# Attention scores from two exact float32 parts on two row halves of the array, late expert weights from a copy, and all orders written anew

## The chip, the core and the metric

The kernel runs on one core of one Trainium2 chip, as one program. The metric is device time in microseconds (us) of one execution. The core has TensorE for matrix products (PE in the profile, with its weight loads as PEld), VectorE (DVE), ScalarE (ACT), GpSimd (POOL), and SyncE (SP), whose queue issues nearly all DMA transfers. Matmul results land in PSUM, which has eight banks of 512 float32 numbers per partition.

## The reference

Input x has 32 sequences of 256 tokens of width 128. Two layers follow each other, with adaptive shift, scale and gate from a small conditioning product per sequence:

- Layer 0: an RWKV block (layernorm, token shift, three projections, the WKV recurrence over time, output projection, then a squared-relu channel mix with 512 hidden units), then a dense MLP 128 to 512 to 128.
- Layer 1: attention with 16 query heads of width 8 and 4 key/value heads, rotary positions, and a softmax over all 256 tokens of the sequence, then a mixture of 8 experts (128 to 512 to 128) of which each token takes two.

The part that the change is about:

```python
scores = jnp.einsum('bthd,bshd->btsh', q, k) * scale
probs = jax.nn.softmax(scores, axis=2)
```

## The kernel before, in words

The work is cut into 16 chunks of two sequences (512 tokens). Each step of a chunk has a name: A and E are the RWKV block, B the dense MLP and the q, k and v projections, C and G attention, R the router, S the slot numbers of the experts and the scatter to them, M the experts, K the gather and the last sum. The tokens of four groups of chunks (5, 5, 4 and 2 chunks) are sorted into tiles of 128 slots, each of which belongs to one expert: 156 tiles in all. The last 62 of them, the late tiles, run as steps W on TensorE (W_t turns four tiles, W_u is the first product, W_d the bias and the second), the others as M.

The order of the work on each engine is written out by hand, as a table ORDER at the file's end: five long lists of step names, one for each engine's queue. Every engine walks its list, and semaphores tie the lists together. An engine never overtakes its own list, so a step that waits holds up everything behind it.

PSUM banks are given out in rings. The ring of attention has the banks 3, 4 and 5, which C_s, C_mt and G_s take in turn; before a step writes its bank, TensorE waits until the bank's last user was read (`vacated`).

Scores need float32 accuracy. Each of q and k is split by ScalarE and GpSimd (B_split, L889, three bf16 copies a chunk, and B_sub, L735, two subtractions between them) into three bf16 parts, stored to scratch (B_stq) and loaded again for one sequence at a time (C_ld), so that each of the 9 pairs of parts of the 8 channels has a row of its own: 72 rows. For every sequence (a unit, 32 in all), TensorE then runs 16 steps C_s: two matmuls of 256 columns each (L1196), one for a head, rows 0 to 71 of the array. VectorE takes the negated row maximum from PSUM (L1581). The maxima are split into three bf16 parts too (C_mp), turned (C_mt), copied out of PSUM by ScalarE (L895) and moved by three small transfers (C_row, L576) into rows 72 to 74 of the q operand, against rows of ones in the k operand. So the second score product, 16 steps G_s of one matmul of 512 columns on 75 rows (L1212), gives the turned scores with the maximum subtracted, of which ScalarE takes the exponential (L903). G_pv (L1228) multiplies the probabilities with v: four heads side by side, each in a tile of 128 rows by 32 columns of the array. Other matmuls that don't take the whole array are the bias products on 3 and 24 rows (L1017, L1041), the k projection (L1178) and C_mt (L1202).

The expert products are L1028 (W_u and M_u: four float32 matmuls of 128 columns), L1041 (the bias, 24 rows, bf16) and L1045 (W_d and M_d: again four float32 matmuls). A float32 matmul stands in the profile as two passes, so four of them are x8. SP loads a tile's weights (514 KB) with L633 from the input wexp. The slot buffers are filled with zeros by four large transfers (Z, L510).

## Time and profile before

| what | value |
|---|---|
| median of 3 runs | 1633.04 us (1629.73 to 1641.36) |
| span of the profiled execution (first to last instruction) | 1622.0 us |
| median of the runs less that span | 11.0 us |
| TensorE busy | 1353.9 us (83%), granted clock 0.909 of full speed |
| VectorE, ScalarE, GpSimd busy | 1095.2, 990.8 and 545.8 us (68%, 61%, 34%) |
| bytes moved | 217.68 MB |

For the profiled execution the profile gives the span; what lies around it is taken from the runs, as in the third row. A row of the timeline gives the start of a group, how long it took to its modelled end, its engine, line, operation and tiles, its form, and how many instructions it merges. "75*128 75x512 bf16" means weights on 75 rows by 128 columns, and a moving operand of 512 columns. Since matmuls are pipelined, their modelled ends lie behind the next one's start; the time from start to start says what a group takes of the engine.

### The profile page before, as it was taken

How to read it: one execution, taken by the hardware profiler on the slowest of the kernel's cores; microseconds unless marked ns; L12 is line 12 of the kernel's file. 1: busy time of each engine (PE TensorE's matmuls, PEld its weight loads, DVE VectorE, ACT ScalarE, POOL GpSimd, SP SyncE). 2: the span in 40 equal slices, each digit the busy share in tenths (PEclk: the TensorE clock that was granted, in tenths of full speed). 3: DMA queues.
4: the chain of work that ended last, by engine and by line, in shares of the span. 5: the costliest groups of instructions: out<-in, count | busy, mean ns of one | idle time of the engine just before them, and what ended most of it. 6: DMA issues, size and time to landing. Idle time of an engine off the chain costs nothing.

```text
span 1622.0 us, 26719 instructions
## 1 busy us (share of the span) xinstructions
PE 1353.9 (83%) x8354; PEld 866.5 (53%) x8354; DVE 1095.2 (68%) x2943; ACT 990.8 (61%) x2295; POOL 545.8 (34%) x589
## 2 busy tenths in 40 slices
PE   3466897889888888999999979899899998998681
PEld 1234454534445444666666644467566754687571
DVE  5568879788989898676876895967755754140113
ACT  1354765667676556877777766567568565555430
POOL 2123222313122475212112256435322134344335
PEclk7677998989999889999999998799999999999885
DMA  4012135142321424454544524256555556788772
GB/s 126 7 36 72 42 114 167 46 132 64 110 77 30 121 83 116 139 157 124 168 134 141 154 87 137 78 164 193 159 169 171 159 166 207 225 275 276 225 244 76
DMA packets 202037, 217.68 MB, mean 134 GB/s; under 512 B 17419, under 2 KB 167526, under 8 KB 199593
## 3 DMA queue, kind: packets, MB, share of 16 engines
q1 hardware_dynamic: 193704, 199.18, 41.0%
q0 software_dynamic: 8192, 16.79, 3.4%
q8 instruction: 68, 1.11, 0.3%
q14 instruction: 73, 0.59, 0.1%
HBM read 161.18 MB, written 53.94 MB: 133 GB/s over the span
## 4 chain that ended last, share of the span: by engine, by line
PE 43%; DVE 21%; issue 11%; ACT 8%; POOL 7%; DMA 6%; SPq 2%; POOLq 0%; ACTq 0%; another core or an unknown queue 0%; DVEq 0%
DVE cmx L1581 6%; PE bank L1228 5%; PE bank L1045 5%; PE bank L1028 5%; PE bank L1212 5%; PE bank L1196 4%; PE bank L1151 3%; PE bank L1124 2%; POOL kg L775 2%; DMA kg<-y_slots,sslot 2%; PE bank L1164 2%; PE bank L1013 2%; POOL bhs L775 2%; ACT wide L903 2%; PE bank L1140 2%
## 5 line engine op out<-in xcount | busy, mean ns | idle before, releaser
L1581 DVE TENSOR_REDUCE cmx<-bank 128x2 f32<-128x512 f32 x512 | 328.7, 684 | 97.4 <-PE bank L1196 89.3
L903 ACT ACTIVATE wide<-bank 128x512 f32<-128x512 f32 x512 | 280.0, 609 | 69.2 <-PE bank L1212 64.6
L1212 PE MATMUL bank<-wide 75*128 75x512 bf16 x512 | 174.9, 407 | 23.2 <-DVE cmx L1581 14.7
L1196 PE MATMUL bank<-wide 72*128 72x256 bf16 x1024 | 176.2, 283 | 20.6 <-DVE cmx L1581 15.6
L756 POOL DMA_INDIRECT x_slots<-sx,sslot x128 | 128.1, 1001 | 111.3 <-issue 46.9
L1196 PEld LDWEIGHTS bank<-wide 72*128 72x128 bf16 x1024 | 92.0, 101 | 124.7 <-issue 48.2
L1228 PE MATMUL bank<-wide,bva 128*32 128x512 f32 x1024 | 146.5, 646 | 9.9 <-ACT wide L903 5.7
L942 ACT ACTIVATE mH<-bank,mW 128x128 f32<-128x128 f32 x376 | 107.0, 371 | 57.8 <-PE bank L1028 50.9
L1028 PE MATMUL bank<-mT,mW 128*128 128x128 f32 x872 | 123.8, 287 | 17.0 <-DMA mW<-in_wexp 7.9
L1028 PEld LDWEIGHTS bank<-mT,mW 128*128 128x128 f32 x872 | 112.6, 199 | 36.3 <-issue 14.7
L775 POOL DMA_INDIRECT kg<-y_slots,sslot x88 | 85.9, 976 | 117.9 <-DMA kg<-y_slots,sslot 35.6
L1212 PEld LDWEIGHTS bank<-wide 75*128 75x128 bf16 x512 | 49.3, 104 | 131.1 <-ACT wide L903 60.1
L1045 PE MATMUL bank<-mW,mH 128*128 128x128 f32 x752 | 109.8, 289 | 0.0
L663 POOL TENSOR_TENSOR brs<-bvar,half 128x4 f32<-128x4 f32 x32 | 33.9, 1058 | 218.2 <-DVE bvar L1297 218.1
L1045 PEld LDWEIGHTS bank<-mW,mH 128*128 128x128 f32 x752 | 91.8, 192 | 6.3
L1151 PE MATMUL bank<-bh,w 128*128 128x512 f32 x128 | 81.2, 720 | 15.1 <-ACT bhs L879 8.0
L735 POOL TENSOR_TENSOR bqk<-bqk,bp 128x768 f32<-128x768 f32 x32 | 54.9, 1715 | 88.9 <-ACT bp L889 88.8
L879 ACT ACTIVATE bhs<-bank,col 128x512 f32<-128x512 f32 x64 | 44.0, 687 | 57.7 <-PE bank L1151 53.4
L949 ACT ACTIVATE mX<-bank 128x128 f32<-128x128 f32 x120 | 33.5, 279 | 73.3 <-PE bank L1045 66.1
L1124 PE MATMUL bank<-axk,fwk 128*128 128x512 f32 x128 | 70.2, 650 | 5.5 <-DVE axk L1300 5.3
L1603 DVE RECIPROCAL crs<-bank 128x16 f32<-128x16 f32 x64 | 16.2, 253 | 84.0 <-PE bank L1234 80.6
L1722 DVE TENSOR_SCALAR kg<-kg,rinfo 128x128 f32<-128x128 f32 x44 | 9.8, 285 | 91.9 <-DMA kg<-y_slots,sslot 91.8
(296 smaller groups left out, 2863.4 us busy)
## 6 DMA issues: line engine op xcount, KB each, us to landing
mW<-in_wexp SPq DMA_DIRECT2D x109, 514.0 KB
wide<-q_parts SPq DMA_DIRECT2D x32, 576.0 KB
inner<-in_wexp SPq DMA_DIRECT2D x31, 514.0 KB
wide<-in_wexp SPq DMA_DIRECT2D x16, 514.0 KB
mX<-x_slots SPq DMA_DIRECT2D x27, 256.0 KB
y_slots<-mX SPq DMA_DIRECT2D x27, 256.0 KB
q_parts<-bp SPq DMA_DIRECT2D x32, 192.0 KB
x_slots<-mH SPq DMA_DIRECT2D x2, 3072.0 KB, 10.9
```

Of the source, the lines that this page charges most:

```text
L756: pool.indirect_dma_start(out=x_slots[GROUP_OF[c]], out_offset=bass.IndirectOffsetOnAxis(ap=sslot[:, c, k, t:t + 1], axis=0), in_=sx[:, c ...
L775: pool.indirect_dma_start(out=kg[z][:, k, t, :], out_offset=None, in_=y_slots[GROUP_OF[c]], in_offset=bass.IndirectOffsetOnAxis(ap=sslot[: ...
L903: act.activation(cP[:, i % 8, :], bank[seat["G_s", i]][:, :], ACT.Exp, scale=SCALE).then_inc(S["c_p"], 1)
L942: act.activation(hidden[z][:, c * P:(c + 1) * P], bank[seat[k]][:, c * P:(c + 1) * P], ACT.Relu, bias=w_[:, FC * P + c:FC * P + c + 1]).th ...
L1028: ins = pe.matmul(ps[:, c * P:(c + 1) * P], weights[w_][:, c * P:(c + 1) * P], mT[:, q % 2, j * P:(j + 1) * P], start=True, stop=True)
L1045: ins = pe.matmul(ps[:, 0:P], hidden[z][:, c * P:(c + 1) * P], weights[w_slot(i)[0]][:, o:o + D], start=False, stop=(c == FC - 1))
L1124: pe.matmul(ps[:, :], fwk[:, j * P:(j + 1) * P], flat(axk[:, :, :]), start=True, stop=True).then_inc(S["e_fk"], 1)
L1151: pe.matmul(ps[:, :], w1[:, j * P:(j + 1) * P], bh[:, :], start=True, stop=True).then_inc(S["b_w1"], 1)
L1196: ins = pe.matmul(ps[:, j * T:(j + 1) * T], cQ[0:SROWS, z, h, tt * P:(tt + 1) * P], cK[0:SROWS, z, h // G, :], start=True, stop=True)
L1212: pe.matmul(ps[:, :], cK[0:KROWS, z, g, sc_ * P:(sc_ + 1) * P], cQ[0:KROWS, z, h0:h0 + 2, :], start=True, stop=True).then_inc(S["c_s2"], 1)
L1228: ins = pe.matmul(CO[32 * g:32 * g + 32, :], bva[:, c % 2, b * 2 + sc_, g, :], cP[:, (4 * i + g) % 8, :], start=(sc_ == 0), stop=(sc_ == 1))
L1581: dve.tensor_reduce(cmx[:, u % 2, tt, 2 * hp:2 * hp + 2], bank[seat["C_s", i]][:, :].rearrange("p (j t) -> p j t", j=2), AX_X, ALU.max, ne ...
```

## The change

- q and k are cut into two float32 parts instead of three bf16 parts. The first keeps the upper 20 bits of the word (VectorE, an AND with a mask, new step B_cut), the second is what is left (GpSimd, one B_sub). The three copies B_split on ScalarE are gone. The row maxima are cut in the same way (C_mp: two operations in place of four).
- The 4 pairs of parts take 32 rows of the array in place of 72 (34 in place of 75 with the maximum). They are read as float32r, one pass per matmul. Heads 0 to 7 lie on rows 0 to 33, heads 8 to 15 on rows 64 to 97. A step C_s or G_s is now a pair: it takes two banks of the ring and alternates matmuls between the two halves. There are 256 of each in place of 512; the number and size of the matmuls is the same, and so are the 512 reduces and 512 exponentials.
- All expert weights (1024 rows of 4112 bytes) are copied once, early, from the input to a scratch tensor w_late (new step I_wl on SP's queue), and the 62 late tiles load theirs from there.
- The q and k operands have an SBUF tensor of their own, qk, in place of a part of wide; the 8 extra weight buffers of the last group lie in both.
- The five lists of ORDER are new.

```diff
+CUTS = 2
+SROWS = CUTS * CUTS * HD
+KROWS = SROWS + CUTS
+HALF = H // 2
+KHALF = KV // 2
+LOW = P // 2
+CUT = -4096.0
...
+PAIRED = ("C_s", "G_s")
...
-            n = banks[k % len(banks)]
-            seat[s, i], before[s, i] = n, had.get(n)
-            had[n] = (s, i)
-            k += 1
+            for j in ((2 * i, 2 * i + 1) if s in PAIRED else (i,)):
+                n = banks[k % len(banks)]
+                seat[s, j], before[s, j] = n, had.get(n)
+                had[n] = (s, j)
+                k += 1
...
-        q_parts = scratch("q_parts", [UNITS * PARTS * P, T], BF16)
-        k_parts = scratch("k_parts", [UNITS * PARTS * HD * KV, T], BF16)
+        q_parts = scratch("q_parts", [UNITS * CUTS * P, T])
+        k_parts = scratch("k_parts", [UNITS * CUTS * HD * KV, T])
+        w_late = scratch("w_late", [EXPERTS * P, WROW])
...
-        bp = sb("bp", [P, PARTS, QK], BF16)
+        bp = sb("bp", [P, CUTS, QK])
+        cutf = sb("cutf", [P, 1])
+        cuti = sb("cuti", [P, 1], I32)
+        cut = cuti[:, :].bitcast(U32)
...
+        qk = sb("qk", [P, NQ * WROW])
+        cQ = qk[:, 0:cQ_ROW].rearrange("p (s h t) -> p s h t", s=2, h=HALF)
+        cK = qk[:, cQ_ROW:cQ_ROW + cK_ROW].rearrange("p (s g t) -> p s g t", s=2, g=KHALF)
+        cQr, cKr = cQ.bitcast(F32R), cK.bitcast(F32R)
...
-        weights += [wide[:, k * WROW:(k + 1) * WROW] for k in range(WIDE)]
+        weights += [qk[:, k * WROW:(k + 1) * WROW] for k in range(NQ)]
+        weights += [wide[:, k * WROW:(k + 1) * WROW] for k in range(WIDE - NQ)]
...
+                    if s == "I_wl":
+                        sp.dma_start(w_late, a["wexp"]).then_inc(S["p_wl"], 16)
...
+                        for o in range(2):
+                            sp.dma_start(cQ[o * LOW:o * LOW + SROWS, z, :, :].rearrange("r h t -> r (h t)"),
+                                         q_parts[i * CUTS * P:(i + 1) * CUTS * P, :]
+                                         .rearrange("(r h) t -> r (h t)", h=H)[:, o * HALF * T:(o + 1) * HALF * T]
+                                         .unsqueeze(1).broadcast_to([CUTS * HD, CUTS, HALF * T])
...
+                        for o in range(2):
+                            sp.dma_start(cQ[o * LOW + SROWS:o * LOW + KROWS, z, :, :].rearrange("r h t -> r (h t)"),
+                                         cmT[o * H:(o + 1) * H, z, :]).then_inc(S[f"c_rows{z}"], 16)
...
-                        sp.dma_start(weights[k], a["wexp"][bass.ds(row, P), :]).then_inc(S[f"m_w{k}"], 16)
+                        if i == LATE_TILE:
+                            sp.wait_ge(S["p_wl"], 16)
+                        sp.dma_start(weights[k], (a["wexp"] if i < LATE_TILE else w_late)[bass.ds(row, P), :]
+                                     ).then_inc(S[f"m_w{k}"], 16)
...
-                        c, k = divmod(i, PARTS - 1)
-                        pool.wait_ge(S["b_p"], PARTS * c + k + 1)
-                        if k:
-                            pool.wait_ge(S["b_r"], i)
-                        pool.tensor_tensor(bqk, bqk, bp[:, k, :], ALU.subtract).then_inc(S["b_r"], 1)
+                        pool.wait_ge(S["b_p"], i + 1)
+                        pool.tensor_tensor(bp[:, 1, :], bqk, bp[:, 0, :], ALU.subtract).then_inc(S["b_r"], 1)
...
-                    if s == "B_split":
-                        c, k = divmod(i, PARTS)
-                        if k:
-                            act.wait_ge(S["b_r"], 2 * c + k)
-                        else:
-                            act.wait_ge(S["b_qk"], 2 * c + 2)
-                            if c:
-                                act.wait_ge(S["b_stq"], 64 * c)
-                        act.activation(bp[:, k, :], bqk, ACT.Copy).then_inc(S["b_p"], 1)
...
+                    if s in PAIRED:
+                        pair = [bank[seat[s, 2 * i + o]] for o in range(2)]
+                        for o in range(2):
+                            vacated(s, 2 * i + o)
+                    elif (s, i) in seat:
...
-                        u, m = divmod(i, MAXES)
+                        u, m = divmod(i, MAXES // 2)
                         z = u % 2
                         if m == 0:
                             pe.wait_ge(S[f"c_ldq{z}"], 64 * (u // 2 + 1))
-                        tt, hp = divmod(m, H // 2)
+                        tt, hp = divmod(m, HALF // 2)
                         for j in range(2):
                             h = 2 * hp + j
-                            ins = pe.matmul(ps[:, j * T:(j + 1) * T], cQ[0:SROWS, z, h, tt * P:(tt + 1) * P],
-                                            cK[0:SROWS, z, h // G, :], start=True, stop=True)
-                        ins.then_inc(S["c_s"], 1)
+                            for o in range(2):
+                                ins = pe.matmul(pair[o][:, j * T:(j + 1) * T],
+                                                cQr[o * LOW:o * LOW + SROWS, z, h, tt * P:(tt + 1) * P],
+                                                cKr[o * LOW:o * LOW + SROWS, z, h // G, :], start=True, stop=True)
+                                if j:
+                                    ins.then_inc(S["c_s"], 1)
...
+                        pp, sc_, g = m // 4, m // 2 % 2, m % 2
                         h0 = g * G + pp * 2
-                        pe.matmul(ps[:, :], cK[0:KROWS, z, g, sc_ * P:(sc_ + 1) * P], cQ[0:KROWS, z, h0:h0 + 2, :],
-                                  start=True, stop=True).then_inc(S["c_s2"], 1)
+                        for o in range(2):
+                            pe.matmul(pair[o][:, :], cKr[o * LOW:o * LOW + KROWS, z, g, sc_ * P:(sc_ + 1) * P],
+                                      cQr[o * LOW:o * LOW + KROWS, z, h0:h0 + 2, :],
+                                      start=True, stop=True).then_inc(S["c_s2"], 1)
...
+                    if s == "B_cut":
+                        dve.wait_ge(S["b_qk"], 2 * i + 2)
+                        if i:
+                            dve.wait_ge(S["b_stq"], 96 * i)
+                        dve.tensor_scalar(bp[:, 0, :].bitcast(U32), bqk.bitcast(U32), cut[:, 0:1], None,
+                                          ALU.bitwise_and).then_inc(S["b_p"], 1)
...
-                        dve.tensor_copy(cmp[:, :, 0, :], x_).then_inc(S["c_mp"], 1)
-                        dve.wait_ge(S["c_mp"], PARTS * i + 1)
-                        v(dve.tensor_tensor(cr1[:, :, :], x_, cmp[:, :, 0, :], ALU.subtract))
-                        v.wait()
-                        dve.tensor_copy(cmp[:, :, 1, :], cr1[:, :, :]).then_inc(S["c_mp"], 1)
-                        dve.wait_ge(S["c_mp"], PARTS * i + 2)
-                        dve.tensor_tensor(cmp[:, :, 2, :], cr1[:, :, :], cmp[:, :, 1, :],
-                                          ALU.subtract).then_inc(S["c_mp"], 1)
+                        dve.tensor_scalar(cmp[:, :, :, 0, :].bitcast(U32), x_.bitcast(U32), cut[:, 0:1], None,
+                                          ALU.bitwise_and).then_inc(S["c_mp"], 1)
+                        dve.wait_ge(S["c_mp"], CUTS * i + 1)
+                        dve.tensor_tensor(cmp[:, :, :, 1, :], x_, cmp[:, :, :, 0, :], ALU.subtract).then_inc(S["c_mp"], 1)
...
-        I_ld A_ld I_ldw I_ldx*16 I_st0 I_ldx*5 A_ldm I_ldx*4 A_ldg I_ldx*4 I_st1 I_ldx*2 A_ld I_ldx B_ldm A_ldm
+        I_ld I_ldw I_ldx*13 A_ld I_ldx*3 I_st0 I_ldx*4 A_ldm I_ldx*9 I_st1 I_ldx A_ldm I_ldx A_ldg A_ld A_ldm
```

Two places show how instructions moved. The first is TensorE's list in the middle of the program, around the channel mix of a chunk (axk, fwk: its first product; mT, mW and mH: expert tiles; ident with bz, ez or cctx: transposes; cos_: attention output; cmp: row maxima; wide with bva: probabilities times v). L1196 (C_s) and L1212 (G_s) read wide. Before:

```order
L1178 MATMUL bank<-bh,wkr 32x256 x2
L1212 MATMUL bank<-wide 128x512 x2
L1196 MATMUL bank<-wide 128x256 x2
L1028 MATMUL bank<-mT,mW 128x128 x4
L1228 MATMUL bank<-wide,bva 32x512 x4
L1212 MATMUL bank<-wide 128x512
L1184 MATMUL bank<-wvT,bh 128x32 x4
L1212 MATMUL bank<-wide 128x512 x2
L1041 MATMUL bank<-eb,which 128x128
L1045 MATMUL bank<-mW,mH 128x128 x4
```

The same kind of place afterwards; L1213 (C_s) and L1234 (G_s) read qk:

```order
L1213 MATMUL bank<-qk 128x256 x4
L1146 MATMUL bank<-fwr,axr 128x128 x4
L1213 MATMUL bank<-qk 128x256 x4
L1140 MATMUL bank<-axk,fwk 128x512
L1213 MATMUL bank<-qk 128x256 x4
L1140 MATMUL bank<-axk,fwk 128x512
L1213 MATMUL bank<-qk 128x256 x4
L1140 MATMUL bank<-axk,fwk 128x512
L1221 MATMUL bank<-ident,cmp 32x128 x2
L1213 MATMUL bank<-qk 128x256 x4
```

Score matmuls still stand singly between float32 groups, now as pairs of steps: four matmuls of 256 columns, or two of 512, at a time.

The second is SP's list where the first maxima go out (C_row, cmT). am, bm, ax, x_b are the loads and stores of other chunks. Before:

```order
L562 DMA wide<-q_parts 72x1x4096
L567 DMA wide<-k_parts 24x1x1024 x3
L524 DMA am<-rows 128x2x256
L541 DMA x_b<-bx 128x4x128
L576 DMA wide<-cmT 1x16x256 x3
```

Afterwards:

```order
L581 DMA qk<-q_parts 32x1x2048
L586 DMA qk<-k_parts 32x1x512
L540 DMA am<-rows 128x2x256
L554 DMA bm<-rows 128x2x128
L523 DMA w_late<-in_wexp 128x8224
L526 DMA x_slots<-mH 1536x1x512
L595 DMA qk<-cmT 2x8x256 x2
```

The copy of the weights is new there, and the first fill with zeros, which stood behind the second C_row, has moved ahead of the first.

## Rows read from the trace of the kernel before

**Rows 1.** The page: span, and busy us of each engine.
```profile
span 1622.0 us, 26719 instructions
PE 1353.9 (83%) x8354; PEld 866.5 (53%) x8354; DVE 1095.2 (68%) x2943; ACT 990.8 (61%) x2295; POOL 545.8 (34%) x589
```
**Rows 2.** Busy time by stretch: PE, PEld, DVE, ACT, POOL, clock, DMA share, GB/s.
```profile
150.00:1384.00 1234.00, 1110.66 (x6922) 679.62 (x6921) 952.80 (x2517) 832.18 (x1848) 410.65 (x434) 0.94 0.42 126
1384.00:1500.00 116.00, 103.01 (x755) 87.86 (x753) 23.28 (x90) 64.50 (x216) 46.24 (x49) 0.97 0.84 263
1500.00:1622.00 122.00, 66.81 (x423) 58.44 (x422) 27.54 (x80) 35.46 (x126) 53.93 (x56) 0.76 0.58 181
```
**Rows 3.** The chain that ended last, by engine.
```profile
PE 43%; DVE 21%; issue 11%; ACT 8%; POOL 7%; DMA 6%; SPq 2%; POOLq 0%; ACTq 0%; another core or an unknown queue 0%; DVEq 0%
```
**Rows 4.** Groups by line: busy us, mean ns | idle before, releaser.
```profile
L1581 DVE TENSOR_REDUCE cmx<-bank 128x2 f32<-128x512 f32 x512 | 328.7, 684 | 97.4 <-PE bank L1196 89.3 <-issue 6.6
L1196 PE MATMUL bank<-wide 72*128 72x256 bf16 x1024 | 176.2, 283 | 20.6 <-DVE cmx L1581 15.6 <-ACT wide L903 2.3 <-issue 1.8
L1212 PE MATMUL bank<-wide 75*128 75x512 bf16 x512 | 174.9, 407 | 23.2 <-DVE cmx L1581 14.7 <-ACT wide L903 5.0 <-DMA wide<-cmT 1.6
L735 POOL TENSOR_TENSOR bqk<-bqk,bp 128x768 f32<-128x768 f32 x32 | 54.9, 1715 | 88.9 <-ACT bp L889 88.8
L889 ACT ACTIVATE bp<-bqk 128x768 bf16<-128x768 f32 x48 | 40.7, 848 | 12.7 <-DVE bqk L1566 8.6 <-POOL bqk L735 3.9
L1486 DVE TENSOR_TENSOR inner<-inner 128x1024 f32<-128x1024 f32 x16 | 19.6, 1225 | 0.6
```
**Rows 5.** Timeline of TensorE in four stretches: start us, us, group.
```profile
702.19 1.05 PE L1028 MATMUL bank<-mT,mW 128*128 128x128 f32 x8
703.08 0.60 PE L1212 MATMUL bank<-wide 75*128 75x512 bf16 x2
703.61 1.06 PE L1228 MATMUL bank<-wide,bva 128*32 128x512 f32 x8
704.61 0.22 PE L1041 MATMUL bank<-eb,which 24*128 24x128 bf16 x1
704.77 1.16 PE L1045 MATMUL bank<-mW,mH 128*128 128x128 f32 x8
705.85 1.07 PE L1228 MATMUL bank<-wide,bva 128*32 128x512 f32 x8
...
708.39 1.02 PE L1107 MATMUL bank<-axv,wv 128*128 128x512 f32 x2
709.25 0.38 PE L1212 MATMUL bank<-wide 75*128 75x512 bf16 x1
709.47 0.95 PE L1257 MATMUL bank<-wrt,rh 128*128 128x8 f32 x8
710.28 0.63 PE L1234 MATMUL bank<-ident,cos_ 128*128 128x128 f32 x4
...
1014.41 0.38 PE L1196 MATMUL bank<-wide 72*128 72x256 bf16 x2
1014.63 1.95 PE L1140 MATMUL bank<-fwv,inner 128*128 128x128 f32 x16
...
1404.63 1.16 PE L1045 MATMUL bank<-mW,axr 128*128 128x128 f32 x8
1405.62 1.06 PE L1028 MATMUL bank<-mT,inner 128*128 128x128 f32 x8
1406.61 0.23 PE L1041 MATMUL bank<-eb,which 24*128 24x128 bf16 x1
```
**Rows 6.** DMA issues: a fill of slots with zeros, KB, us to landing.
```profile
x_slots<-mH SPq DMA_DIRECT2D x2, 3072.0 KB, 10.9
```
**Rows 7.** TensorE's waits for weights among the late tiles, from the timeline.
```profile
1537.81 2.05 PE L1028 MATMUL bank<-mT,mW 128*128 128x128 f32 x8 [7.35 <-DMA mW<-in_wexp]
1577.09 2.05 PE L1028 MATMUL bank<-mT,wide 128*128 128x128 f32 x8 [4.50 <-DMA wide<-in_wexp]
```

485 lines of the change are left out of this document (234 added, 251 removed).

## The prediction

> **What bounds the kernel now.** I read the page's busy times first [rows 1], then busy times by stretch [rows 2], the chain that ended last [rows 3], the costliest groups [rows 4], and then, for most of the work, the timeline of TensorE [rows 5].
>
> TensorE (PE) is busy for 83% of the span. By stretch this is sharper: from 150 to 1384 us, where the attention, the two dense layers and the first expert tiles run together, PE is busy 1110.66 of 1234 us (0.90), VectorE 952.80 (0.77), ScalarE 832.18 (0.67), at a granted clock of 0.94, so nearly all of it at the 2.4 GHz level. From 1384 us on only expert tiles and their gathers are left, 238 us long, and there PE shares the bound with transfers. The chain says the same: PE has 43% of it, VectorE 21%. So the question is what the change does to PE's time in a stretch in which nine tenths of any microsecond that PE gains or loses shows. VectorE's largest item is the row maximum over the scores, 512 reduces of 684 ns, and the change leaves all 512.
>
> Busy time overstates a pipelined matmul, so I price matmuls from start to start [rows 5]. Two score matmuls of 256 columns start 0.22 us before what follows (1014.41 to 1014.63), one of 512 columns also takes 0.22 (709.25 to 709.47). A float32 matmul of 512 columns is two passes, 0.86 us (708.39 to 709.25). Eight float32 passes of 128 columns take 0.89 (702.19 to 703.08). Eight float32 passes with only 8 columns take 0.81 (709.47 to 710.28), so there it is the weight load of 128 four-byte columns that sets the pace: 0.10 us each, hidden when the matmul is that long.
>
> The same rows show a price that the diff does not mention. A matmul that takes another part of the array than the one before it costs extra. Two score matmuls before the probability product, whose tiles are 32 columns wide, take 0.53 and not 0.43 (703.08 to 703.61). The 128 columns of the expert bias, on 24 rows, take 0.16 and not 0.05 (704.61 to 704.77). L1028 before such a bias takes 0.99 and not 0.89 (1405.62 to 1406.61). So a switch costs 0.10 us. And L1045, the float32 group right behind a switch, takes 0.99 with no other switch near (1404.63 to 1405.62), and 1.08 with one behind it (704.77 to 705.85): its first load had not been pulled ahead, another 0.10. A bf16 group behind a switch pays almost nothing.
>
> **The change part by part.**
>
> *Score matmuls.* 512 steps C_s and 512 steps G_s, 0.22 us each, are 112.6 + 112.6 = 225.3 us of PE. Afterwards 256 pairs of each run on row halves. If the halves run side by side and a float32r column costs what a bf16 one does, a pair takes one step's 0.22 us, and 112.6 us go. Nothing in the trace runs on row halves. The nearest row is the probability product: eight passes of 512 columns on four column tiles take 1.00 us (703.61 to 704.61), where at 0.43 one after another they would take 3.4. So tiles do run side by side. The bounds are -112.6 (full overlap) and 0 (none); a rate of float32 passes, 0.43 per 512 columns, with overlap also gives 0. I take -112.6.
>
> By the Trainium skill (TensorE: Matmul & The Clock Gate, Measured speedup vs the span model) four row tiles of 512 columns reached 3.07 times, not 4. By that share of the ideal a pair would gain a factor of about 1.5, and the term would be an estimated -78 in place of -112.6. No run here shows it.
>
> *Switches.* Before, a score step took 72 or 75 rows, the whole array, like its float32 neighbours. Now C_s takes 32 rows and G_s 34, thus another part of the array than each other and than nearly everything else. Counted over the compiled programs, PE changes the part 711 times before and 1314 times after: 603 more at 0.10 us are +60.3. Behind a switch stands a float32 group 377 times before and 695 times after: 318 more at 0.10 are +31.8. A float32r score group stands there 461 times. Its first load is four-byte like the one that costs 0.10, but a single pass on one row half, and for bf16 the price was near 0.01; bounds 0 and 0.10, I take the middle, 0.05: +23. Sum +115. The float32 row is the nearer one in bytes, so this term has more room upwards.
>
> Of loads, the trace and the skill differ. The rows of 128-column float32 passes (0.89 for eight, with loads of 0.10 each) show loads hidden under matmuls on the very same rows. The Trainium skill (TensorE: Matmul & The Clock Gate, The mechanism) says that a load overlaps a running matmul only when the row group differs. If only that rule held, putting the operands on halves would be an extra gain; by the rows, that gain is there already, and I give it nothing.
>
> PE's balance is -112.6 + 115 = +2.5 us, and nine tenths of it count: +2. That is the core of this forecast: what the halves give, the drains between forms take back.
>
> *PSUM banks.* A pair needs two of the ring's three banks and waits for both. While VectorE reduces the second bank of a pair (684 ns), the next pair (0.22 to 0.40 us) fits in. Behind a waiting pair stand all of PE's later steps, and who waits is VectorE; covered by the reduce, 0. Without that cover it would be some 0.2 us for each of 256 pairs at most, +50.
>
> *Splitting q and k.* 48 copies of 848 ns leave ScalarE (40.7 us), 16 of 32 subtractions leave GpSimd (27 us), and 16 ANDs over 768 words join VectorE: between 0.6 and 1.2 us each by the 1225 ns of 1024 elements [rows 4], about 16 us. All three engines have slack in the stretch. GpSimd waited 88.8 us for ScalarE's copies, with the layernorm and residual steps of other chunks queued behind it; one such wait per chunk of two goes. Bounds -15 and +10 (VectorE has 281 idle us, but the AND sits in its queue ahead of reduces); I take -5.
>
> *Transfers.* By their shapes the q and k loads are about as large as before (640 KB in place of 720 per unit; the stores grow by as much), and SP issues as many. New is the copy of all expert weights, 4.1 MB, on SP's queue, and right behind it a zero fill, both now ahead of the first C_row, without which the first G_s and all of PE behind it wait. A fill of 3072 KB lands in 10.9 us [rows 6], so both take 14.6 + 10.9 = 25.5 us. The 16 reduces before C_row take 10.9 of it. Bounds 0 and 15; I take +5, since PE is at its lightest there.
>
> *The tail.* 62 late tiles at 0.99 + 0.16 + 0.99 = 2.14 us of PE are 133 of the 238 us. Much of the rest is waits, among them 7.35 and 4.50 us for weights [rows 7]. The new order runs up to three W_u before their W_d, so that ScalarE's work lies beside PE. The weights come from another buffer of the same layout, for which I see no reason to be faster. Bounds -30 and +10; I take -12.
>
> Sum: +2 - 5 + 5 - 12 = -10 us on a span of 1622.0, thus 1612. The median of the runs shown is 1633.04, 11.0 us above the span; with the same 11.0 around it, **1623 us**.
>
> **The rivals.**
>
> *Slower: the four-byte loads bind.* Place: PE's queue, in the score pairs. A C_s pair has four loads of 128 columns but only 0.22 us of matmul if halves overlap. At the 0.10 us of row 709.47 they take 0.40, +0.18 for 256 pairs = +46, and a first load behind a switch at 0.10 is +23 more. Nine tenths of 69 are 62: 1623 + 62 = 1685. Against it: loads of the small column tiles ran ahead of each other. It decides for slower once such loads add 29 us to PE's time (0.9 of that is the 26 from 1623 to 1649).
>
> *Faster: switches between full array and row tiles cost little, or PE spends them where it waits for VectorE anyway.* Then of the +115 some 25 are left, and nine tenths of 90 are 81: 1623 - 81 = 1542, rounded to 1545. For it: VectorE's reduces, 684 ns per step against 0.22 of PE, already set the pace in long runs of C_s. Against it: the bias on 24 rows is a row tile, and it paid the full 0.10 on both sides.
>
> *The halves don't run side by side (the change does not do what it says).* Then 112.6 us stay, and the switches come on top: 1623 + 101 = 1724. Against it stands the probability product.
>
> **How the numbers follow.** A measurement tells about 1% here, 16 us. The forecast has 0.40, with its own range 1600 to 1650; slower by loads 0.27, faster 0.25, no overlap 0.08. Faster than 1617: the 0.25 and some four tenths of the forecast, 0.42. Slower than 1649: nearly all of the two slow cases and a little of the forecast, 0.34. Within: 0.24. The range reaches both neighbours, 1545 to 1690, and leaves out the case without overlap.
>
> **What would show it.** Right: two score matmuls of a pair starting within a few hundredths of a microsecond; 0.10 us more in front of each run of them; PE's busy share in the middle stretch near 0.9 still. Wrong: pairs at 0.40 or more (loads), or starts one matmul apart (no overlap), or no gap at switches (faster). GpSimd's wait for the copies should be gone, and the first G_s should come some 5 us late.

## The result, and the profile after

The changed kernel takes 1807.86 us (median of 4 runs, 1806.19 to 1811.47) against 1631.38 us for the kernel before beside it: a ratio of 1.1064, with a 95% interval of 1.1029 to 1.11. The forecast was 1623 us, and its range ended at 1690. In a later comparison the ratio was 1.1082 (1.1032 to 1.1131).

The page of the changed kernel: span, busy us of each engine, the granted clock in 40 slices, and the chain by engine.

```profile
span 1809.6 us, 27057 instructions
PE 1462.8 (81%) x8354; PEld 914.8 (51%) x8354; DVE 1108.3 (61%) x2897; ACT 969.9 (54%) x2247; POOL 526.8 (29%) x575
PEclk6677887888868587999999897798888898799796
PE 56%; DVE 11%; ACT 9%; issue 9%; DMA 7%; POOL 5%; SPq 2%; another core or an unknown queue 1%; POOLq 0%; ACTq 0%; DVEq 0%
```

TensorE (PE) now has 56% of the chain in place of 43 [rows 3], and 109 us more busy time for the same number of matmuls [rows 1]. The busy time by stretch (us of the stretch, then PE, PEld, DVE, ACT, POOL, clock, DMA share, GB/s) says where:

```profile
150.00:1560.00 1410.00, 1223.80 (x6895) 732.18 (x6898) 966.79 (x2468) 810.63 (x1796) 387.68 (x416) 0.85 0.38 114
1560.00:1700.00 140.00, 111.97 (x799) 92.22 (x791) 28.49 (x103) 70.53 (x232) 52.97 (x55) 0.89 0.80 248
1700.00:1810.00 110.00, 58.54 (x414) 52.09 (x414) 23.89 (x70) 34.31 (x121) 50.82 (x53) 0.78 0.59 174
```

Against [rows 2] the middle stretch grew from 1234 to 1410 us, 176 of the 188 us that the span grew. Its granted clock fell from 0.94 to 0.85. There are two levels, 1.2 and 2.4 GHz, so 0.85 means that three tenths of the time lay at the lower one, where it had been about one tenth. What comes after grew by 12 us.

The groups that answer to [rows 4], busy us and mean ns of one, then idle time before and its releaser:

```profile
L1615 DVE TENSOR_REDUCE cmx<-bank 128x2 f32<-128x512 f32 x512 | 330.4, 685 | 142.8 <-PE bank L1213 131.4
L1213 PE MATMUL bank<-qk 32*128 32x256 f32 x1024 | 141.8, 356 | 64.0 <-DVE cmx L1615 40.8
L1234 PE MATMUL bank<-qk 34*128 34x512 f32 x512 | 149.6, 578 | 45.5 <-ACT wide L915 22.5
L1251 PE MATMUL bank<-wide,bva 128*32 128x512 f32 x1024 | 167.9, 737 | 1.0 <-DVE cxo L1649 0.6
```

TensorE idles 109.5 us before score matmuls (64.0 + 45.5) where it idled 43.8 (20.6 + 23.2 [rows 4]). The two engines that read the scores wait longer for it all the same: VectorE's reduces 131.4 us in place of 89.3, and ScalarE's exponentials 142.6 us in place of 64.6. Everyone waits more for everyone. Now the timeline of TensorE in the changed kernel (start us, us, group), at the full clock as in [rows 5]:

```profile
1002.62 0.50 PE L1234 MATMUL bank<-qk 34*128 34x512 f32 x2
1003.05 1.12 PE L1167 MATMUL bank<-bh,w 128*128 128x512 f32 x2
1004.02 1.05 PE L1040 MATMUL bank<-mT,mW 128*128 128x128 f32 x8
1005.00 0.49 PE L1234 MATMUL bank<-qk 34*128 34x512 f32 x2
1005.43 1.07 PE L1251 MATMUL bank<-wide,bva 128*32 128x512 f32 x8
```

and the same view in a stretch at the low clock, where the last column is idle time and its releaser:

```profile
623.24 1.92 PE L1167 MATMUL bank<-bh,w 128*128 128x512 f32 x2
625.08 0.79 PE L1213 MATMUL bank<-qk 32*128 32x256 f32 x4
626.75 0.79 PE L1213 MATMUL bank<-qk 32*128 32x256 f32 x4 [0.87 <-DVE cmx L1615]
627.47 2.08 PE L1167 MATMUL bank<-bh,w 128*128 128x512 f32 x2
629.47 0.79 PE L1213 MATMUL bank<-qk 32*128 32x256 f32 x4
631.14 0.80 PE L1213 MATMUL bank<-qk 32*128 32x256 f32 x4 [0.88 <-DVE cmx L1615]
```

In the first of the two stretches a pair takes 0.43 us from start to start (1002.62 to 1003.05). That alone would also fit two matmuls of 0.22 us one after the other. But the two records of this pair start 0.003 us apart (1002.623 and 1002.626), and a single step on one half takes as long as a pair. This is oldsingles, a variant described below, at the full clock:

```profile
926.67 0.50 PE L1236 MATMUL bank<-qk 34*128 34x512 f32 x1
927.10 1.13 PE L1188 MATMUL bank<-bh,wqT 128*128 128x512 f32 x2
```

With a change of the array part on both sides, the median is 0.431 us for a pair (69 of them, at the full clock) and 0.428 for a single step there (68). So the halves do run side by side, and the second is almost free. Of the 0.43 us the columns take 0.22. Pairs with a change before them and none behind take 0.35 (0.347, ten pairs of C_s), so about 0.09 belongs to the change behind and 0.12 to the first load behind a change.

The stretch at the low clock shows both losses at once. L1167 takes 1.84 us (623.24 to 625.08) in place of 0.97 (1003.05 to 1004.02), and a pair that follows a pair stands still for 0.87 us, with VectorE's reduce as the releaser: one bank of the ring is free, but the other that the pair needs was written by the pair just before it and has not been read yet.

To compare kernels I use one table, worked out from each kernel's timeline over the stretch from 150 us to the last C_s. All times are in us, and each ratio is against the kernel before on the same chip; the variants are described in the next section. Work is start-to-start time without the idle time that the rows name. Work at full clock prices each kind of matmul at its mean in those 5 us slices in which the clock was fully granted; cold is the rest. The clock is the mean over the slices. Priced record by record, the column of work at full clock moves by up to 8 us, so smaller differences in it mean nothing.

| kernel | ratio to before (95%) | last C_s | clock | idle | at full clock | cold |
|---|---|---|---|---|---|---|
| before | 1 | 1367 | 0.947 | 116 | 1044 | 57 |
| changed | 1.106 (1.103 to 1.110) | 1551 | 0.851 | 183 | 1057 | 160 |
| oldfull | 1.003 (1.000 to 1.006) | 1376 | 0.948 | 93 | 1080 | 53 |
| oldsingles | 1.096 (1.086 to 1.107) | 1511 | 0.866 | 74 | 1139 | 147 |
| fewrows | 1.092 (1.083 to 1.101); 1.069 for the traced run | 1478 | 0.861 | 66 | 1100 | 161 |
| crows32 | 1.029 (1.020 to 1.038) | 1417 | 0.916 | 90 | 1083 | 92 |
| crows64 | 1.019 (1.011 to 1.028) | 1410 | 0.932 | 97 | 1088 | 73 |
| fill128 | 1.001 (0.998 to 1.003) | 1366 | 0.964 | 107 | 1070 | 39 |
| fill32 | 1.013 (1.009 to 1.016) | 1393 | 0.933 | 95 | 1076 | 70 |
| fullown | 1.052 (1.043 to 1.061) | 1463 | 0.931 | 155 | 1086 | 72 |
| fullspread | 1.077 (1.067 to 1.086) | 1498 | 0.915 | 169 | 1083 | 95 |
| fullrows | 1.085 (1.079 to 1.091) | 1500 | 0.914 | 175 | 1079 | 95 |
| fullrows16 | 1.072 (1.067 to 1.078) | 1496 | 0.913 | 197 | 1053 | 96 |
| ownbank | 1.098 (1.092 to 1.103) | 1524 | 0.855 | 129 | 1082 | 161 |
| filled | 1.100 (1.091 to 1.109) | 1534 | 0.914 | 126 | 1159 | 99 |
| latecopy | 1.115 (1.108 to 1.122) | 1559 | 0.849 | 193 | 1050 | 165 |

For fewrows the trace is of its fastest run (1744.00 us, 1.069 of before), while 1.092 also counts three runs in the slow state (1770.23 to 1794.41), and the one slow run of oldsingles (1791.52) is left out.

Of the 184 us by which the last C_s came later in the changed kernel, 13 are work at full clock, 67 idle time, 103 the low clock.

### The profile page after: what moved, and what is told of

It reads as the page before. It is cut to its first block, busy times and chain, and to the rows that moved or that the text cites. A ratio compares the mean times of both kernels' runs of the same rounds, so it can differ in the third digit from the quotient of the medians.

```text
span 1809.6 us, 27057 instructions
## 1 busy us (share of the span) xinstructions
PE 1462.8 (81%) x8354; PEld 914.8 (51%) x8354; DVE 1108.3 (61%) x2897; ACT 969.9 (54%) x2247; POOL 526.8 (29%) x575
## 4 chain that ended last, share of the span: by engine, by line
PE 56%; DVE 11%; ACT 9%; issue 9%; DMA 7%; POOL 5%; SPq 2%; another core or an unknown queue 1%; POOLq 0%; ACTq 0%; DVEq 0%
PE bank L1251 6%; PE bank L1057 6%; PE bank L1040 6%; PE bank L1213 5%; PE bank L1234 5%; PE bank L1167 4%; PE bank L1140 4%; PE bank L1180 3%; DVE cmx L1615 3%; PE bank L1156 3%; ACT wide L915 2%; PE bank L1025 2%; PE bank L1188 2%; POOL bhs L798 2%; PE bank L1257 1%
## 5 line engine op out<-in xcount | busy, mean ns | idle before, releaser
L1615 DVE TENSOR_REDUCE cmx<-bank 128x2 f32<-128x512 f32 x512 | 330.4, 685 | 142.8 <-PE bank L1213 131.4
L915 ACT ACTIVATE wide<-bank 128x512 f32<-128x512 f32 x512 | 280.1, 599 | 148.5 <-PE bank L1234 142.6
L1213 PE MATMUL bank<-qk 32*128 32x256 f32 x1024 | 141.8, 356 | 64.0 <-DVE cmx L1615 40.8
L1234 PE MATMUL bank<-qk 34*128 34x512 f32 x512 | 149.6, 578 | 45.5 <-ACT wide L915 22.5
L1213 PEld LDWEIGHTS bank<-qk 32*128 32x128 f32 x1024 | 87.2, 205 | 168.0 <-issue 72.8
L1251 PE MATMUL bank<-wide,bva 128*32 128x512 f32 x1024 | 167.9, 737 | 1.0 <-DVE cxo L1649 0.6
L1234 PEld LDWEIGHTS bank<-qk 34*128 34x128 f32 x512 | 56.7, 212 | 167.4 <-ACT wide L915 74.9
L1040 PE MATMUL bank<-mT,mW 128*128 128x128 f32 x872 | 131.4, 298 | 4.9 <-DMA mW<-in_wexp 2.2
L1057 PE MATMUL bank<-mW,mH 128*128 128x128 f32 x752 | 120.3, 308 | 0.0
L1167 PE MATMUL bank<-bh,w 128*128 128x512 f32 x128 | 93.3, 819 | 14.7 <-ACT bh L893 8.2
L1057 PEld LDWEIGHTS bank<-mW,mH 128*128 128x128 f32 x752 | 101.0, 209 | 6.8
L1140 PE MATMUL bank<-axk,fwk 128*128 128x512 f32 x128 | 77.9, 712 | 7.0 <-DVE axk L1323 6.0
L1180 PE MATMUL bank<-w,bhs 128*128 128x128 f32 x512 | 67.9, 291 | 0.0
## 6 DMA issues: line engine op xcount, KB each, us to landing
x_slots<-mH SPq DMA_DIRECT2D x2, 3072.0 KB, 18.2
```

Of the source, the lines that this page charges most:

```text
L915: act.activation(cP[:, i % 8, :], bank[seat["G_s", i]][:, :], ACT.Exp, scale=SCALE).then_inc(S["c_p"], 1)
L1040: ins = pe.matmul(ps[:, c * P:(c + 1) * P], weights[w_][:, c * P:(c + 1) * P], mT[:, q % 2, j * P:(j + 1) * P], start=True, stop=True)
L1057: ins = pe.matmul(ps[:, 0:P], hidden[z][:, c * P:(c + 1) * P], weights[w_slot(i)[0]][:, o:o + D], start=False, stop=(c == FC - 1))
L1140: pe.matmul(ps[:, :], fwk[:, j * P:(j + 1) * P], flat(axk[:, :, :]), start=True, stop=True).then_inc(S["e_fk"], 1)
L1167: pe.matmul(ps[:, :], w1[:, j * P:(j + 1) * P], bh[:, :], start=True, stop=True).then_inc(S["b_w1"], 1)
L1180: ins = pe.matmul(ps[:, t * P:(t + 1) * P], bhs[:, c, t * P:(t + 1) * P], w2[:, c, :], start=False, stop=(c == FC - 1 and t == NT - 1))
```

## The experiments

### Taking the few rows away: fullrows and oldfull

fullrows keeps everything of the changed kernel but the array half. Each of its matmuls reads both halves, so its scores are sums of two heads and only its time is of use:

```diff
-    cQr[o * LOW:o * LOW + SROWS, z, h, tt * P:(tt + 1) * P],
-    cKr[o * LOW:o * LOW + SROWS, z, h // G, :], ...
+    cQr[0:LOW + SROWS, z, h, tt * P:(tt + 1) * P],
+    cKr[0:LOW + SROWS, z, h // G, :], ...
```

> The changed kernel in its own order, banks, transfers and splits; only the score matmuls no longer take row halves: C_s reads rows 0 to 95 and G_s rows 0 to 97 of the same operands (the rows between are set to zero), so every score matmul takes the whole array and a pair gives the sum of two heads twice. Left out are thus separate scores for the two halves. Gone: the overlap of the halves and the switches around score steps. Still there: the wait for two banks, the early copy, the new lists. In the changed kernel TensorE idled 184 us in its stretch 150 to 1560 against 118 before, and its work took 1228 us there where it would take about 1061 at full clock. If few rows make the chip grant the low clock (rows theory), the granted clock of the stretch returns to 0.93 or more and the time falls to 1640 to 1690. If the waits for two banks and the order do it (bank and order theories), the clock stays at 0.88 or less and the time stays above 1770.

The ratio was 1.085 (1755.67 us). The clock rose from 0.851 to 0.914, so rows have a hand in it. But idle time stayed (175 us), and clock and time both came out between the two forecasts. I then put the same operands on the old lists, first on halves, then on the whole array:

```diff
-PAIRED = ("C_s", "G_s")
+PAIRED = ()
...
-                        u, m = divmod(i, MAXES // 2)
+                        u, m = divmod(i, MAXES)
+                        m, o = divmod(m, 2)
```

> The changed kernel's operands and halves on the order of the kernel before: each C_s and G_s is again one step that takes one bank and one head pair on one half, 512 of each, in the old lists (B_split taken out, B_cut put behind B_k, the copy of the weights moved behind the seventh G_st). Only 248 of 512 partners stand side by side there, so about 264 overlaps of 0.22 us are lost and 65 runs of score steps are added: about 70 us more TensorE work than in the changed kernel. If the new lists and the two-bank wait cost the 176 us, the clock is back at 0.93 or more, idle time near 118 us, and the time is 1660 to 1720, faster than the changed kernel in spite of that work. If few rows bring the low clock, the clock is 0.87 or less and the time is 1800 or more.

> As oldsingles (old lists, one bank a step, float32r operands from two parts), but each score matmul reads rows 0 to 95 or 0 to 97 and so takes the whole array; separate scores of the two halves are left out. In oldsingles TensorE hardly idled (74 us in the middle stretch) and yet the clock was 0.866. Rows theory: with whole-array score matmuls the clock is back at 0.94 or more on the same lists; the work at full clock is some 52 us above the kernel before (0.157 in place of 0.133 us for 256 columns, 0.319 in place of 0.266 for 512, as in fullrows), so the time is 1.02 to 1.045 of before. If the clock hangs on something else that both share (operands, splits, transfers), it stays below 0.89 and the ratio above 1.07.

The stretch from 150 us to the last C_s in oldsingles (columns as above):

```profile
150.00:1511.00 1361.00, 1282.73 (x6850) 771.90 (x6850) 947.95 (x2447) 800.87 (x1785) 379.55 (x412) 0.87 0.38 116
```

and in oldfull:

```profile
150.00:1376.00 1226.00, 1127.05 (x6849) 767.91 (x6848) 941.83 (x2445) 794.50 (x1782) 382.00 (x412) 0.95 0.43 128
```

oldsingles took 1777.79 us, ratio 1.096, with TensorE busy 1282.73 of 1361 us (0.94) and less idle time than before, and still the clock was 0.87. The time lies between its two forecasts, the clock at the one of few rows. oldfull, the same lists with as many matmuls, took 1636.19 us: 1.003, even below its forecast, at a clock of 0.948. So on the old lists the use of few rows costs about 9%, of which 94 us are the clock (147 against 53 cold) and about 60 are work at full clock for changes of the array part and the loads behind them (1139 against 1080). The rest of the new way to compute scores (two exact parts, fewer splits) costs nothing that counts. The new lists were not needed to lose most of the time.

### The kernel before on few rows: fewrows, crows32, crows64

Here loads are two-byte, lists and banks those of before:

```diff
-    cQ[0:SROWS, z, h, tt * P:(tt + 1) * P], cK[0:SROWS, z, h // G, :]
+    cQ[64:SROWS, z, h, tt * P:(tt + 1) * P], cK[64:SROWS, z, h // G, :]
...
-    cK[0:KROWS, z, g, sc_ * P:(sc_ + 1) * P], cQ[0:KROWS, z, h0:h0 + 2, :]
+    cK[64:KROWS, z, g, sc_ * P:(sc_ + 1) * P], cQ[64:KROWS, z, h0:h0 + 2, :]
```

> The kernel before, all bf16 and in its own order, but C_s and G_s read only rows 64 to 71 and 64 to 74: eight of the 72 product rows, and the three of the maximum. Left out are the products of the other 64 rows. Nothing runs side by side, loads stay two-byte, lists and banks are those of before. Added by hand count: some 720 changes of the array part at 0.10 us, and up to 380 first loads behind one at 0.10, so 70 to 110 us of TensorE. Rows theory: on top of that the granted clock falls from 0.94 to 0.88 or less and the ratio is 1.09 or more. Without an effect of rows on the clock the ratio is 1.03 to 1.065 and the clock 0.93 or more, since TensorE is then busier than before.

In the traced run the ratio was 1.069 and the clock 0.861, with TensorE busy 0.95 of the stretch and idle for only 66 us. So the kernel before, with its bf16 operands, lost most of what oldsingles lost by this edit alone. The clock is where the rows theory put it; the ratio of the traced run is below the 1.09 that it asked for. The added work at full clock is 56 us, the added cold time 104. But fewrows adds changes of the array part too: 1350 in the trace, in place of 711. crows32 and crows64 make nearly the same changes (1115 and 1163 in their traces) with different numbers of rows (`cQ[0:32, ...]`, `cK[0:32, ...]` or 64, in C_s alone):

> The kernel before with its own lists, banks and bf16 operands; only C_s reads rows 0 to 31 in place of 0 to 71 (left out are the products of the other 40 rows in the row maximum), G_s is unchanged. It changes the array part before and behind every run of C_s. To be read against crows64, which makes the same changes with twice the rows. If the rows in use bring the low clock, the clock of the middle stretch lies clearly under crows64's, by 0.03 or more, and the ratio is 1.04 to 1.07. If the changes of part (drains) bring it, both have the same clock and the same ratio within 0.5%.

> As crows32, but C_s reads rows 0 to 63: half the array. The same changes of the array part as crows32 in number and place. Rows theory: clock 0.92 or more and ratio 1.02 to 1.035 (some 35 us of changes and first loads, little clock). Drain theory: the same clock and ratio as crows32.

On one chip, crows32 took 1681.70 us (1677.15 to 1689.56) and crows64 1668.65 (1666.41 to 1670.32). The stretch of crows32, where the groups show C_s as 32*128:

```profile
150.00:1417.00 1267.00, 1172.16 (x6848) 674.35 (x6846) 949.16 (x2496) 826.53 (x1830) 405.08 (x428) 0.92 0.41 121
```

and of crows64, where they show it as 64*128:

```profile
150.00:1410.00 1260.00, 1158.48 (x6847) 671.62 (x6845) 948.07 (x2496) 825.95 (x1828) 405.18 (x427) 0.93 0.42 122
```

Work at full clock is the same (1083 and 1088), the clock is not (0.916 and 0.932). Over the whole program it was 0.877 to 0.886 in the four runs of crows32 and 0.898 to 0.900 in those of crows64. The step of 0.016 is half of what I had asked for, and their intervals against before overlap, though the times of the runs side by side do not. So with the changes held, fewer rows mean a lower clock, which the theory of drains alone had ruled out. The work added in both, about 40 us, is the price of the changes. The step from 72 rows and 0.947 to 64 rows and 0.932 brings the changes along with it, and no run tells how much of it they cause; so how the clock's fall to 0.86 in fewrows divides between rows and changes stays open.

### Extra matmuls in idle places: fill128, fill32, filled

181 matmuls of 512 columns that nobody reads, at 51 idle places of the kernel before, written as steps F in TensorE's list, make fill128. fill32 differs from fill128 in one thing:

```diff
-    pe.matmul(bank[seat[s, i]][:, :], identb[:, :], identb[:, :]...
+    pe.matmul(bank[seat[s, i]][:, :], identb[0:32, :], identb[0:32, :]...
```

> The kernel before, with 181 bf16 matmuls of 512 columns on all 128 rows that nobody reads, at 51 places of TensorE's list in which the trace of before shows it idle for 0.45 us or more with its bank free (66 us idle in all; the fillers are some 40 us at full clock). If work on many rows holds the clock up, the clock of the middle stretch rises from 0.947 to 0.96 or more, part of the 57 us that the low clock costs comes back, and the ratio is 0.98 to 0.995: this version could beat both. If the idle time is not where the clock is lost, the ratio is 1.00 to 1.02.

> As fill128, the same number of fillers at the same places, but each on rows 0 to 31 only. Rows theory: these do not hold the clock up: the clock of the middle stretch stays at 0.95 or less, under that of fill128 by 0.01 or more, and the ratio is 0.5% or more above fill128's (the changes of the array part add up to 0.2 us at each of 51 places, 10 us, on top). If it is TensorE's being busy at all that counts, both have the same clock.

The stretch of fill128:

```profile
150.00:1366.00 1216.00, 1102.73 (x6948) 672.60 (x6949) 944.86 (x2487) 821.32 (x1826) 401.15 (x427) 0.96 0.43 125
```

and of fill32:

```profile
150.00:1393.00 1243.00, 1141.62 (x6965) 689.12 (x6964) 945.83 (x2492) 824.34 (x1828) 401.38 (x427) 0.93 0.42 122
```

On 128 rows the clock rose from 0.947 to 0.964, on 32 rows it fell to 0.933, though TensorE was busier than without any (1141.62 of 1243 us against 1096.37 of 1217). Over the whole program the clock was 0.917 to 0.931 in the runs of fill128, 0.899 to 0.903 in those of fill32 and 0.901 to 0.915 without fillers, so the two kinds are told apart, while the fall on 32 rows is small. The Trainium skill (TensorE: Matmul & The Clock Gate, What's actually happening) says that the clock gate is set by how busy the engine has been recently. These rows, and oldsingles, show that busy time alone does not settle it: the same number of matmuls on 32 rows left the clock 0.031 lower than on 128. fill128 won back 18 us of cold time and spent 26 on the fillers: 1.0006, nothing gained, though I had forecast a gain if the clock rose. (At 1.0125, fill32 also pays for 95 more changes of the array part, some 10 us of its 22.)

The same idea in the changed kernel, three fillers where a pair follows a pair and one where a single step stands between:

```diff
-                        for o in range(2):
-                            vacated(s, 2 * i + o)
+                        vacated(s, 2 * i)
+                        for _ in range(fillers[s, i]):
+                            pe.matmul(pair[0][:, :], identb[:, :], ...)
+                        vacated(s, 2 * i + 1)
```

> The changed kernel with bf16 matmuls of 512 columns that nobody reads, between the waits for the first and the second bank of a pair: three where a pair follows a pair at once (71 places), one where one step stands between (219 places). That is about 95 us of added TensorE work at full clock, part of it in idle time. If idling of TensorE brings the low clock, the granted clock of the middle stretch rises from 0.85 to 0.93 or more, and the time stays within 40 us of the changed kernel or falls, since the 107 us lost to the clock pay for the work. If few rows bring it, the clock rises by 0.03 at most and the time grows by 50 us or more.

The clock rose to 0.914 and 61 us of cold time went, but the fillers are 102 us of work: the ratio was 1.100, about as without them (1.106). I had left out that they also run where nothing was idle. Neither forecast had both the clock and the time right: the clock rose by 0.06, twice what the rows theory allowed, but not to the 0.93 of the other.

### The wait for two banks, and the lists: ownbank, fullown, fullspread

ownbank waits for each bank just ahead of the half that writes it:

```diff
-                        for o in range(2):
-                            vacated(s, 2 * i + o)
...
+                        for o in range(2):
+                            vacated(s, 2 * i + o)
+                            for j in range(2):
```

> The changed kernel, but in each pair the first half's matmuls wait for their own bank only and are issued before the wait for the second bank. TensorE is held up as long as before behind the pair, but VectorE and ScalarE get the first half by as much earlier as the second bank is late. If the wait for both banks at once is the cause, 30 to 100 us come back and the clock rises by 0.03 or more. If the cause is the rows or the lists, the time moves by less than 20 us.

Idle time fell by 54 us (183 to 129), work at full clock rose by 25 (the two halves' matmuls no longer alternate), and the clock, which should have risen by 0.03, did not move. The time was 1778.23 us, 30 less than the changed kernel, but on a chip on which the kernel before was 12 us faster too. By the ratios (1.098 and 1.106) it is 0.9%, some 15 us, and the two intervals touch: under the 30 us that I had asked for. fullown does this without the halves, fullspread moves 190 of the second steps behind their next neighbour:

> As fullrows (the changed kernel's lists, whole-array score matmuls), but the two steps of a pair stand side by side as single steps, each waiting for its own bank. Operands and matmuls are those of oldfull (1.003), so what is left over oldfull is the lists, the early copy and nothing else; what it gains on fullrows (1.085) is the wait for both banks at once. If the pair's wait is the main part, the ratio is 1.03 or less; if the lists are, it is 1.06 or more. ownbank did the same on halves and gained 0.9%, so I expect 1.07.

> As fullown, but in 190 of the 256 pairs the second step is moved behind the expert, RWKV or dense step that follows the pair, as most score steps stand in the lists of before. If the lists of TensorE cost time because two score steps in a row outrun the three banks (VectorE needs 684 ns for each and ScalarE 600), TensorE's idle time falls from the 175 us of fullrows to 110 or less and the ratio to 1.03 or less. If the lists cost it in another way (what waits for what at a larger scale), it stays within 1% of fullown.

fullown gained 3% on fullrows (1.052 against 1.085, in different comparisons), between what I had written for the wait and for the lists. So the wait for both banks costs about 1% on halves and 3% on the whole array. fullspread lost most of what fullown had won (1.077), which neither of its forecasts had. Moving a step behind its neighbour delays its reader instead: VectorE's reduces wait 123.3 us for TensorE in place of 95.3, and ScalarE's exponentials 138.0 in place of 95.4. "The lists outrun the banks" is no good description of what is wrong with them. What is left between fullown and oldfull, 1.052 against 1.003, is the lists and the copy. Of the 87 us between their last C_s, 62 are idle time and 19 the clock. The waits of TensorE show part of the idle time. In fullown (us in all, times, longest us):

```profile
PE bank L1218 <- DVE cmx L1621: 19.2, 19, 3.5
PE bank L1069 <- DMA mX<-x_slots: 18.7, 1, 18.7
PE bank L1218 <- DMA qk<-k_parts: 16.1, 6, 5.3
PE bank L1057 <- ACT mH L958: 14.9, 24, 1.5
```

and the answering ones of oldfull:

```profile
PE bank L1218 <- DVE cmx L1621: 13.1, 20, 1.3
PE bank L1240 <- DVE cmx L1621: 12.0, 10, 2.8
PE bank L1057 <- ACT mH L958: 7.3, 9, 1.2
```

With the new lists the loads of k come too late six times (16.1 us), which TensorE never waits for in oldfull, and expert steps wait twice as long for ScalarE's relu (14.9 against 7.3). The 18.7 us for a slot load fall at 1614 us, behind the last C_s, where fullown takes no longer than oldfull (256 and 263 us). No run exchanges the list of one engine alone, so which list carries the 5% stays open.

### Four-byte loads, and the copy: fullrows16, latecopy

fullrows16 is fullrows with the score matmuls reading the upper two bytes of each word:

```diff
-        cQr, cKr = cQ.bitcast(F32R), cK.bitcast(F32R)
+        cQr = qk[:, 0:cQ_ROW].bitcast(BF16).rearrange(...)[:, :, :, :, 1]
```

> As fullrows, but the score matmuls read the upper two bytes of each operand word as bf16, so that their loads are two-byte; left out are the low bits of each part and the separate scores of the halves. Against fullrows this takes away the part of a score step that the four-byte loads set: 0.157 to 0.133 and 0.319 to 0.266 us, 52 us in all. If TensorE's work counts in this order, the ratio falls from 1.085 to 1.055 or less. If what is left of fullrows against before is the two-bank wait and the order, TensorE only waits more (idle above 200 us in the middle stretch) and the ratio stays above 1.07.

Work at full clock fell by 26 us, idle time rose by 22, ratio 1.072: nearly as the second theory had it, most of the work saved on TensorE turned into waiting in these lists. A 256-column score matmul took 0.157 us with four-byte and 0.130 with two-byte operands, one of 512 columns 0.319 and 0.265 (means at full clock).

latecopy moves the copy of the weights to a later place in SP's list:

> The changed kernel with the copy of the expert weights moved behind the seventh G_st on SP's queue, far from the start. If the early copy and the zero fill behind it delay the first C_row and so everything behind, 5 to 15 us come back and the first G_s starts near 180 us in place of 188.6. If the copy is hidden, nothing moves by more than 5 us.

Nothing came back: 1.115, and the first G_s started at 190.0 us in place of 188.6. To know how much chips and hours differ, I ran the changed kernel once more:

> The changed kernel once more, unchanged: a ratio of 1.10 to 1.115. If it comes out at 1.11 or more, moving the copy (latecopy, 1.115) made no difference; at 1.10, moving it cost 1%.

1.1082: the intervals of the two overlap (1.1081 and 1.1131 are their near ends), so moving the copy made no difference that can be told.

## Why the prediction was wrong

By the steps of its own sum:

- **The balance of TensorE's work (+2.5 us): right within what can be told.** At full clock it was +13 (1044 to 1057), about 10 when priced record by record. The overlap (-112.6) is as forecast: 0.431 us for a pair and 0.428 for a single step with the same neighbours. For it, the Trainium skill (TensorE: Matmul & The Clock Gate, Measured speedup vs the span model) had led to an estimated factor of about 1.5 for a pair; here it is 2.0 (twice 0.428 in 0.431).
- **One piece of that balance was too small.** The first load of a score group behind a change costs 0.12 us, where I took 0.05 and a bound of 0.10; over 461 groups that is some 32 us more. The sum held within 10 us all the same, so other pieces came out lower by some 20 us. They are not taken apart here, and that much of the agreement is luck.
- **Neighbours paid as forecast.** Eight passes of W_u or M_u take 0.893 us with no change of part near, 0.986 with one behind them, 0.995 with one before them and 1.088 with both (medians at full clock).
- **The granted clock: the step that failed.** "at a granted clock of 0.94, so nearly all of it at the 2.4 GHz level" was carried over without a word as if a property of the stretch. It fell to 0.85, which is 103 of the 184 us. No term and no rival held it. fewrows (0.861) and oldsingles (0.866) show that putting the score matmuls on few rows is enough to bring it down on the old lists, with TensorE busier than before; oldfull (0.948) shows that it comes back on the whole array. What part of it the rows themselves have and what part the changes of array part is not known.
- **PSUM banks (0, bound +50): wrong.** "covered by the 684 ns reduce" looked at VectorE, which indeed has work meanwhile; TensorE does not. Two pairs in a row need four banks of a ring of three, so TensorE stands until a reduce is through, and everything behind the pair stands with it (0.87 us in the rows at the low clock). With a wait for each bank by itself 54 us of idle time went (ownbank), against 67 that had been added; in time it is 0.9%, and 3% on the whole array (fullown).
- **The lists: priced only by their changes of part and in the tail.** With the same score matmuls and banks they cost 5% (fullown against oldfull, the early copy included). I had not asked whether each engine's list still fits the others'.
- **Splitting (-5): consistent, but not measured by itself.** GpSimd's wait for the copies is gone (L758 waits 43.0 us for VectorE, where it waited 88.8 for ScalarE), and oldfull, which has this part of the change, is at 1.003.
- **Transfers (+5): the sign right, the cause wrong.** The first G_s came 10 us later (178.4 to 188.6), and a fill landed in 18.2 us, against 10.9 [rows 6]. But moving the copy away changed nothing: in latecopy the fill had landed at 172.0 us, and the first C_row went out only at 182.7. The delay is there before the copy is even issued, at 160.9 us: the first C_s starts at 159.1 us in place of 151.3, behind loads of q and k that SP issues 9.5 us later (150.3 in place of 140.9).
- **The tail (-12): wrong.** The waits for weights [rows 7] are gone and one of 6.97 us for a slot load came in; from the last C_s to the end it is 259 us where it was 255, and not 12 less.

The sum of terms is no sum: few rows alone (oldsingles) take 9%, the lists with the two-bank wait alone (fullrows) 8.5%, both together 10.6%. My reading is that slower matmuls cost less where TensorE waits for others, and the other way round; the 26 us of work and 22 of waiting in fullrows16 fit that. The rivals were of the right sign only in "the four-byte loads bind"; its mechanism is real on the whole array (26 us in fullrows16), but it isn't what cost the time. None of the variants beats the kernel before: oldfull and fill128 come level with it, and oldfull does not give the scores of separate heads.

## What to carry to other kernels

Before packing small matmuls side by side, look at the granted clock of the stretch and ask what the array's use will be afterwards: matmuls on about a quarter of the rows or fewer went with a clock of 0.86 even where TensorE was busier (oldsingles, fewrows), and every other matmul in the stretch paid for it. Price an operation that takes two buffers at once by the time until the second is free, not by its own length. And when a change rewrites the order too, run its arithmetic on the old order first: here that one run (oldfull, 1.003) showed that the number format and the splits were harmless and the form on few rows was not.

## What the hardware showed that I had not expected

- In these runs the clock went with the rows that matmuls use, not only with TensorE's busy time: 0.964 with 181 fillers on 128 rows, 0.947 with none, 0.933 with the same fillers on 32; 0.932 with C_s on 64 rows, 0.916 on 32.
- In oldfull 32 of the 96 rows of a C_s hold zeros in the k operand, and the clock was 0.948 against 0.947 with 72 rows of data; so the zeros did not visibly pull it down.
- Two row halves overlap almost fully also with four-byte operands read as float32r: 0.431 us for a pair, 0.428 for one half alone. The changes of part around it and the first load behind one cost more than the columns themselves: about 0.10 + 0.09 + 0.12 us, against 0.22.
